# Graph attention on one core: scores of two units in a row as 64-row matmuls from the split halves, and all six units' probabilities turned by DMA

## What is computed

```python
h = relu(layernorm(x))
q, k, v = h @ Wq + bq, h @ Wk + bk, h @ Wv + bv      # split into 6 heads of 64
scores = q @ k.T / sqrt(64) + where(adj, 0, -9e15)    # 256 x 256 per head
ctx = softmax(scores) @ v                             # heads joined again: 256 x 384
out = x + ctx @ Wf + bf
```

## Time and profile before

| | us |
|---|---|
| median of 3 runs | 651.73 (651.4 to 652.34) |
| the profiled execution, its own time | 649.83 |
| its span, first to last instruction | 648.0 |
| granted TensorE clock, mean | 0.997 |

### The profile page before, as it was taken

One profiled execution on the slowest core, in us unless ns is written; L12 is line 12 of the kernel. 1 busy time (PEld: TensorE's weight loads), 2 busy tenths in 40 slices (PEclk: granted clock), 3 DMA queues, 4 the chain that ended last, 5 costly groups with the idle time before them and its releaser, 6 DMA issues.

```text
span 648.0 us, 18229 instructions
## 1 busy us (share of the span) xinstructions
PE 623.6 (96%) x6678; PEld 511.9 (79%) x6678; DVE 493.0 (76%) x1545; ACT 517.5 (80%) x1166; POOL 423.5 (65%) x465
## 2 busy tenths in 40 slices
PE   8787999999999999999999999999999999999985
PEld 7465888888888888888888888888888888888853
DVE  6777787787778778777777877777787777877764
ACT  3558888888888888888888888888888888888872
POOL 3556677676667767666776766677676676767531
PEclk9999999999999999999999999999999999999999
DMA  8317677777667668866777697687867877766554
GB/s 251 89 34 148 154 142 147 167 156 155 158 158 144 150 150 168 154 158 157 136 159 160 155 156 160 155 143 152 153 158 165 149 164 134 165 133 127 130 127 91
DMA packets 207690, 95.84 MB, mean 148 GB/s; under 512 B 152817, under 2 KB 207602, under 8 KB 207602
## 3 DMA queue, kind: packets, MB, share of 16 engines
q1 hardware_dynamic: 206400, 94.68, 69.5%
q10 hardware_dynamic: 1202, 0.01, 0.1%
HBM read 17.05 MB, written 12.58 MB: 46 GB/s over the span
## 4 chain that ended last, share of the span: by engine, by line
PE 87%; issue 3%; DMA 2%; POOL 2%; SPq 2%; DVE 2%; ACT 1%; POOLq 0%; ACTq 0%; DVEq 0%
PE ring L859 18%; PE ring L861 18%; PE ring L860 18%; PE scores L920 6%; PE scores L921 6%; PE probs_t L930 4%; PE ctx L948 3%; PE ring L960 3%; PE ctx L950 3%; PE ctx L949 3%; PE ring L875 3%; DMA w_raw<-in_L_gnn_Wk_dram 1%; SPq L305 1%; DMA heads<-split 1%; SPq L297 1%
## 5 line engine op out<-in xcount | busy, mean ns | idle before, releaser
L406 POOL TENSOR_TENSOR p_rows<-probs,p_rows 128x512 f16<-128x512 f32 x128 | 148.5, 1160 | 143.8 <-ACT p_rows L509 143.8
L643 DVE CUSTOM_DVE_ANT_0 logits<-scores,mask,logit_unscale 128x256 f32<-128x256 f32 x384 | 170.5, 482 | 90.6 <-PE scores L921 90.6
L499 ACT ACTIVATE probs<-logits,raised 128x256 f32<-128x256 f32 x384 | 174.2, 500 | 6.2
L859 PE MATMUL ring<-h_hi,w_hi 128*128 128x256 f16 x576 | 157.1, 273 | 0.4 <-DVE w_lo L741 0.4
L861 PE MATMUL ring<-h_hi,w_lo 128*128 128x256 f16 x576 | 157.0, 272 | 0.0
L860 PE MATMUL ring<-h_lo,w_hi 128*128 128x256 f16 x576 | 156.9, 272 | 0.0
L390 POOL TENSOR_TENSOR split<-qk,split 128x512 f16<-128x512 f32 x96 | 111.7, 1164 | 42.1 <-DVE split L667 42.1
L521 ACT ACTIVATE qk<-ring,qk_bias_s,qkv_ratio 128x256 f32<-128x256 f32 x192 | 97.2, 557 | 5.4 <-PE ring L861 2.6
L948 PE MATMUL ctx<-v_hi,p_cols 128*128 128x65 f16 x768 | 89.1, 194 | 10.2 <-DMA p_cols<-p_rows 5.6
L920 PE MATMUL scores<-heads 128*128 128x256 f16 x384 | 94.3, 273 | 3.9 <-DMA heads<-split 3.9
L921 PE MATMUL scores<-heads 128*128 128x256 f16 x384 | 94.2, 273 | 0.0
(11 more groups left out here) (97 smaller groups left out, 1406.9 us busy)
## 6 DMA issues: line engine op xcount, KB each, us to landing
heads<-split SPq DMA_DIRECT2D x192, 96.0 KB, 2.2
x_in<-in_x_dram SPq DMA_DIRECT2D x32, 384.0 KB, 3.5
heads<-split SPq DMA_DIRECT2D x192, 64.0 KB, 2.1
out_dram<-result SPq DMA_DIRECT2D x64, 192.0 KB, 2.3
adj_in<-in_adj_dram SPq DMA_DIRECT2D x32, 64.0 KB, 2.3
p_cols<-p_rows SPq DMA_TRANSPOSE x128, 3.2
w_raw<-in_L_gnn_Wq_dram SPq DMA_DIRECT2D x1, 576.0 KB, 5.7
w_raw<-in_L_gnn_Wk_dram SPq DMA_DIRECT2D x1, 576.0 KB, 7.5
```

The source lines that it names most:

```text
L406: pool.tensor_tensor(p_rows[u][:, 1], probs[u % 3][:], p_rows[u][:, 0], ALU.subtract).then_inc(p_lo_ready, 1)
L499: act.activation(probs[u % 3][:, a], logits[u % 3][:, a], ACT.Exp, bias=raised[u % 3][:, a:a + 1], scale=-1.0).then_inc(probs_ready, 1)
L643: dve.tensor_tensor_reduce(out=logits[u % 3][:, a], in0=score_bank[u % 2][:, a * S:(a + 1) * S], in1=mask[b.parity][:, t], scale=logit_uns ...
L859: pe.matmul(out_ap, a_hi, m_hi, start=first, stop=False)
```

## The change

The four stacking DMAs a pair, the `heads` buffers and their zeros go. `split` gets a second copy by parity of the batch. `scores` now works for a group of two units (g = 0, 1, 2: units 2g and 2g+1) and is issued in `attend(0)`, `attend(2)` and `attend(4)`: for each unit three products (q_hi k_hi, q_hi k_lo, q_lo k_hi), each as two matmuls of 64 rows, head 0 from partitions 0 to 63 into bank 0, head 1 from partitions 64 to 127 into bank 1. A unit's parity picks the half of the bank. The group waits until VectorE has read all the units of the group before. All six units are split before they are turned, and turned by DMA; the transposes on TensorE, ScalarE's and VectorE's work on `pt_bank` go, and ScalarE's `probs_hi` of units 0 and 3 now stands right behind their `exps`.

```diff
-PE_UNITS = (0, 3)
+    GROUPS = UNITS // 2
-        split = [sb(f"split{j}", [P, 4, S], F16) for j in range(C)]
-        heads = [sb(f"heads{p}", [P, HEADS, 3, S], F16) for p in range(2)]
+        split = [[sb(f"split{p}_{j}", [P, 4, S], F16) for j in range(C)] for p in range(2)]
@@ SyncE
-            def place_heads(b, j):
-                wait(sp, qk_hi_ready, b.count(C, j + 1))
-                wait(sp, qk_lo_ready, b.count(C, j + 1))
-                for a in range(2):
...
-                    sp.dma_start(dst[own], src[own, 1:4]).then_inc(heads_placed[j], 16)
-                    sp.dma_start(dst[other, 0:2], src[own, 0:3:2]).then_inc(heads_placed[j], 16)
             def transpose_probs(b, u):
-                if u in PE_UNITS:
-                    return
-                wait(sp, p_lo_ready, b.count(len(DMA_UNITS), nth_dma(u)))
+                wait(sp, p_lo_ready, b.count(UNITS, u + 1))
@@ GpSimd
             def probs_lo(b, u):
-                if u in PE_UNITS:
-                    return
-                wait(pool, p_hi_ready, b.count(len(DMA_UNITS), nth_dma(u)))
+                wait(pool, p_hi_ready, b.count(UNITS, u + 1))
@@ ScalarE
             def exps(b, u):
-                if u < 3:
-                    if (b + -1).exists():
-                        probs_read(act, b + -1, u + 3)
-                else:
-                    probs_read(act, b, u - 3)
+                wait(act, p_lo_ready, b.count(UNITS, u - 2))
             def probs_hi(b, u):
-                if u in PE_UNITS:
-                    wait(act, pt_ready, b.count(len(PE_UNITS), nth_pe(u)))
-                    act.activation(p_cols[u][:, 0].rearrange("p a s q -> p (a s q)"), pt_bank[:],
-                                   ACT.Copy).then_inc(pt_hi_ready, 1)
-                    return
@@ VectorE
-                wait(dve, scores_ready, b.count(UNITS, u + 1))
+                wait(dve, scores_ready, b.count(GROUPS, u // 2 + 1))
-                        out=logits[u % 3][:, a], in0=score_bank[u % 2][:, a * S:(a + 1) * S],
+                        out=logits[u % 3][:, a], in0=score_bank[a][:, u % 2 * S:(u % 2 + 1) * S],
-            def probs_lo(b, u):
-                if u not in PE_UNITS:
-                    return
...
@@ TensorE
-            def scores(b, u):
-                t, j = u // C, u % C
-                if t == 0:
-                    wait(pe, heads_placed[j], b.count(4 * 16, 4 * 16))
-                wait(pe, logits_ready, b.count(2 * UNITS, 2 * u - 2))
...
+            def scores(b, g):
+                for u in (2 * g, 2 * g + 1):
+                    if u < C:
+                        wait(pe, qk_hi_ready, b.count(C, u + 1))
+                        wait(pe, qk_lo_ready, b.count(C, u + 1))
+                wait(pe, logits_ready, b.count(2 * UNITS, 4 * g))
+                for u in (2 * g, 2 * g + 1):
+                    t, tile = u // C, split[b.parity][u % C]
+                    for n, (q, k) in enumerate(((1, 2), (1, 3), (0, 2))):
+                        for a in range(2):
+                            own = slice(D * a, D * a + D)
+                            mm = pe.matmul(score_bank[a][:, u % 2 * S:(u % 2 + 1) * S],
+                                           tile[own, q, t * P:(t + 1) * P], tile[own, k],
+                                           start=(n == 0), stop=(n == 2))
                 mm.then_inc(scores_ready, 1)
-            def transpose_probs(b, u):
...
@@ TensorE, attend(u)
-                    if here:
-                        scores(b, u)
+                    if here and u % 2 == 0:
+                        scores(b, u // 2)
...
-                    if here and u - 1 in PE_UNITS:
-                        transpose_probs(b, u - 1)
```

More of the change, by code:

```diff
@@ L61, in gnn_attention @@
     UNITS = QT * C
-    DMA_UNITS = [u for u in range(UNITS) if u not in PE_UNITS]
+    GROUPS = UNITS // 2
     LAG = 4
@@ L254, in cycles @@
                 cycle(Batch(k))
[L256 to L264, removed]
-            if u in PE_UNITS:
-                wait(eng, pt_ready, b.count(len(PE_UNITS), nth_pe(u)))
-            else:
-                wait(eng, p_lo_ready, b.count(len(DMA_UNITS), nth_dma(u)))
         x_v = x.rearrange("b (t p) h -> b p t h", p=P)
@@ L576, in cycle @@
                     exps(b, 0)
+                    probs_hi(b, 0)
                 if here:
@@ L585, in cycle @@
                     v_hi_part(b, 1)
-                if here:
-                    probs_hi(b, 0)
                 if front:
@@ L600, in cycle @@
                     exps(b, 3)
+                    probs_hi(b, 3)
                 if front:
@@ L606, in cycle @@
                     probs_hi(b, 4)
-                    probs_hi(b, 3)
                 if b.k == 0:
@@ L750, in _ @@
                 dve.memset(v_hi[p][:, :, :, D:V1], 1.0).then_inc(ones_ready, 1)
-                for a in range(2):
-                    other = slice(D - D * a, 2 * D - D * a)
-                    dve.memset(heads[p][other, a:HEADS:2, 2], 0.0).then_inc(zeros_placed, 1)
             layer_stats(Batch(0), (0, 1))
@@ L816, in cycle @@
                     qk_hi_part(b + 1, 0)
-                if here:
-                    probs_lo(b, 0)
                 if before:
@@ L843, in cycle @@
                     weights_lo(3, 8)
-                if here:
-                    probs_lo(b, 3)
                 if before:
@@ L909, in project_v @@
                     mm.then_inc(v_ready, 1)
-            def scores(b, u):
-                t, j = u // C, u % C
-                if t == 0:
-                    wait(pe, heads_placed[j], b.count(4 * 16, 4 * 16))
-                wait(pe, logits_ready, b.count(2 * UNITS, 2 * u - 2))
-                for a in range(2):
-                    h = heads[b.parity][:, 2 * j + a]
-                    q = h[:, 0, t * P:(t + 1) * P]
-                    o = score_bank[u % 2][:, a * S:(a + 1) * S]
-                    pe.matmul(o, q, h[:, 1], start=True, stop=False)
-                    mm = pe.matmul(o, q, h[:, 2], start=False, stop=True)
-                mm.then_inc(scores_ready, 1)
@@ L924, in transpose_probs @@
-            def transpose_probs(b, u):
-                wait(pe, pt_lo_ready, b.count(len(PE_UNITS), nth_pe(u) - 1))
-                for a in range(2):
-                    wait(pe, probs_ready, b.count(2 * UNITS, 2 * u + a + 1))
-                    for s in range(QT):
-                        o = (a * QT + s) * P
-                        mm = pe.transpose(pt_bank[:, o:o + P], probs[u % 3][:, a, s * P:(s + 1) * P], ident[:])
-                mm.then_inc(pt_ready, 1)
+            def scores(b, g):
[12 more added lines that the diff above has]
+                                           start=(n == 0), stop=(n == 2))
+                mm.then_inc(scores_ready, 1)
@@ L933, in apply_probs @@
             def apply_probs(b, u):
                 t, j = u // C, u % C
-                if u in PE_UNITS:
-                    wait(pe, pt_lo_ready, b.count(len(PE_UNITS), nth_pe(u)))
-                else:
-                    wait(pe, p_placed[u], b.count(16, 16))
+                wait(pe, p_placed[u], b.count(16, 16))
                 if u == 0:
@@ L1001, in _ @@
             pe.wait_ge(peaks_joined, 1)
-            spread_peaks(pt_bank, slice(4, 5))
+            spread_peaks(peak_bank, slice(4, 5))
             def cycle(b):
@@ L1061, in cycle @@
                     project_v(b + 1, 1)
-            pe.wait_ge(zeros_placed, 4)
             cycles(cycle)
```

34 lines of the change are left out of this document (6 added, 28 removed).

## The result

The kernel after takes 620.2 us (median, 619.76 to 622.47) where the kernel before took 651.57 us (650.65 to 652.34) beside it on the same chip. The ratio is 0.9527, 95% interval 0.9505 to 0.955. The profiled execution took 620.36 us, its span is 618.4. Forecast were 619.5 us in a range of 602 to 640: it holds. By its own time the profiled execution fell by 29.5 us (649.83 to 620.36), not by the 32.2 of the sum. The other 1.9 us of the 31.4 between the medians come from which execution was profiled: that of before lay 1.7 us under its median of 651.57, that of after 0.2 above its own. The granted clock goes with this: of the 19 executions of before that were timed beside experiments 1 to 4, the five with a mean clock of 0.997 took 649.2 to 649.7 us, and those with 0.992 took 650.7 to 652.6.

The account below looks back on a forecast made before the run. TensorE's matmul stream was taken as the bound: 18.88 - 0.94 - 0.65 + 0.60 = 17.89 us a batch. Over 29 batches 28.7, plus 2.5 and 1.0, is 32.2 us less: median 651.73 to 619.5, range 602 to 640.

Parts of the forecast that it names:

- the 32.2 of the sum: Whole profiled execution: 28.7 us less from 29 full cycles, 2.5 from the fill, 1.0 from the drain; 649.83 becomes 617.6.
- TensorE's sum: TensorE's matmul stream in a full batch: 18.88 - 0.94 - 0.65 + 0.60 = 17.89 us.
- The turns: Transposes of two units a batch leave TensorE, 0.47 us each: -0.94 us a batch.
- A pair: Two 64-row score matmuls on different array halves overlap wholly, costing one 0.109 us: 18 pairs, -0.65 us a batch.
- The ways in and out: TensorE switching to 64 rows and back around each score group: 0.10 us each, six a batch, +0.60 us.
- the scores' forecast (-0.05): TensorE's new scores a batch: -0.65 us from overlapping matmuls and +0.60 for switching to 64 rows and back.
- The chain: ScalarE and VectorE steps from turned context to `h_lo`: 6.1 us with the semaphore, just fits TensorE's path of 6.15.
- the rival of free switches: On TensorE, switching to 64 rows costs nothing; the ScalarE-VectorE path to `h_lo` binds at 17.45 us a batch, 606.7 us; chance 0.22.
- ScalarE, GpSimd, VectorE: Their load a batch: ScalarE about 16.2 us, GpSimd 15.40, both under 17.89; VectorE loses work; GpSimd and VectorE cost 0.
- another engine: ScalarE and GpSimd, in fixed order behind each other, lose 2 us to waits: 18.4 us a batch, 634 us; chance 0.06.
- SyncE and DMA: DMA queue: twelve stacking DMAs a batch go, two transposes come; some 3 us stay before `apply_probs`, cost 0.
- Fill and drain: First and last batches: fill -2.5 us (bounds -7 and -1), drain -1 us (bounds 0 and -2).

Follow-up runs that it names:

- experiment 1: The kernel before with all six units turned by DMA, stacked heads and 128-row scores kept: 674.65 us, ratio 1.0372.
- experiment 2: The kernel before with the new 64-row scores and no stacking DMAs, units 0 and 3 still turned on TensorE: 650.87 us, ratio 1.000.
- experiment 3: The kernel after with each unit's three matmuls of head 0 first, then the three of head 1: 621.22 us, ratio 0.9565.
- experiment 4: The kernel after with each group's second unit behind `apply_probs`, so six switches to 64 rows and back a batch: 651.32 us, ratio 1.0013.
- experiment 5: The kernel after with one unused VectorE operation of 0.55 us ahead of `h_lo_part`: 638.14 us, ratio 0.9803.
- experiment 6: The kernel after with scores in two groups of three units a batch, two switches in and out instead of three: 632.2 us, ratio 0.9704.
- experiment 8: GpSimd normalises batch 2's x behind the first cycle's mask and lo halves: kernel after 620.71 us; two groups of three units 630.01, with unit 5 masked early 613.79.
- the groups of three with the mask early: The kernel after with scores in two groups of three units and VectorE masking unit 5 right behind unit 4: 616.31 us, ratio 0.9482.

## Why the prediction was right

- **TensorE's sum.** 17.89 us a batch forecast, 17.93 measured. The turns gave 0.94 (experiment 2 to after). A pair costs 0.109, whole overlap. The ways in and out cost 3 x (0.096 + 0.093) = 0.57, forecast 0.60 from the single-row matmuls: a hole seen on float32 with one row held for float16 with 64. The first step of a group is 0.01 longer, 0.03 a batch. The steps inside `apply_probs` add up to 2.02 us a batch where they were 1.99, 0.03 more. With the 0.03 that the ways cost less, that is, to 0.01, what lies between the scores' forecast (-0.05) and experiment 2 (-0.01).
- **The chain.** That a chain of 6.1 us "just fits" into a path of 6.15 was the sharpest step: room of 0.05 forecast, 0.08 measured, 0.6 and 0.56 for before. From the last matmul that turns the context, the chain takes 6.14 us before and 6.15 after, while TensorE's own way to the q, k product fell from 6.76 to 6.29. Experiments 4, 5 and 6 show that it is the next bound, as the rival of free switches said.
- **ScalarE, GpSimd, VectorE.** 16.2, 15.40 and cost 0 forecast; the window has 15.87 and 15.23, and no TensorE wait. The rival "another engine" didn't come.
- **SyncE and DMA.** Right for the whole change, as TensorE has no wait for `p_placed`. But "The stacking itself was on no path in the full cycles" hides what experiment 1 shows. Without the removal of the stacking DMAs the two added transposes would have cost more than they give. The prediction looked at the new load of this queue only as a sum of both parts.
- **Fill and drain.** This is the term that was mis-sized: -2.5 and -1.0 forecast. Measured: the first full `transpose_h` at 71.76 against 73.30, -1.5. From the last listed one to the end, 62.43 us against 64.88, less two shorter cycles, -0.55. Together with 0.04 x 29 of the period that is about the 2.7 us between 32.2 and 29.5.
- **Luck in the median.** The profiled time was forecast at 617.6 and came at 620.36, 2.7 us off. The forecast of the median, 619.5, is only 0.7 off because it added the 1.9 us by which the profiled run of before lay under its median, and after has no such distance. That cancels 2.0 of the 2.7.

What the drain fell short by is the clock, as a second trace shows. Here is one window of 3.4 us in the kernel after and in experiment 3, whose scores of the last batch start at the same distances from its last `transpose_h` to within 0.02 us:

```profile
599.00:602.40 3.40, 3.40 (x26) 1.81 (x23) 1.83 (x9) 3.27 (x8) 2.23 (x2) 0.50 0.83 146
```

```profile
599.00:602.40 3.40, 2.46 (x33) 1.70 (x33) 3.12 (x14) 3.27 (x9) 1.74 (x3) 1.00 0.80 172
```

The kernel after is at 0.50, the 1.2 GHz level, after TensorE was busy for 6.48 of the 9 us before; experiment 3 stays at 1.00 there after 7.43 of 9. From the start of the last `transpose_h` to the end are 44.5 us in the first and 43.3 in the second. In the kernel before they were 46.0, with the clock at 1.00 to the end, and 0.95 of the difference is one shorter cycle. So the drain saves 1.7 us without that stretch and 0.5 with it, where 1.0 was forecast.

What took the place of the removed waits in the fill: TensorE's waits from 20 to 75 us, and a window of that stretch with its clock.

```profile
PE ctx L872 <- DMA p_cols<-p_rows: 4.7, 2, 3.1
PE ring L791 <- DVE w_lo L680: 3.4, 1, 3.4
```

```profile
45.00:50.00 5.00, 3.33 (x22) 1.85 (x21) 4.15 (x13) 4.49 (x9) 5.00 (x5) 0.60 0.87 181
```

The waits for heads (3.9 us in the earlier trace rows) are gone, those for turned probabilities grew from 2.3 to 4.7, and a wait of 3.4 for `w_lo` is new. GpSimd has two lo halves more in the first cycle and is busy for all 5 us of the window, but it was that before too, so that they are the cause is argued; with GpSimd's order changed (experiment 8) the wait for turned probabilities left this list and the time stayed. The clock is at 0.60 in this window, in part at the 1.2 GHz level, after TensorE was busy for only 1.93 of the 5 us before. The kernel before had 1.00 in the same window, after 4.23 of 5. How much of the 1.0 us missing in the fill is the clock stays open.

## What to carry to other kernels

A wait that vanishes from a profile may have been replaced by room of 0.08 us. Look at the distance from the last producer's end to the consumer's start and compare it with the distance when the consumer really waits (0.06 here): that tells what the next saving can bring. Count an edit also by what it frees on a shared queue. The scores alone gave nothing, the turn alone lost 3.7%, both together gained 4.7%. Where two engines feed a chain, bring the chain's own step ahead of work that nobody waits for before shortening the bound engine: the groups of three lost 0.39 us a batch without that and won 0.21 with it.

## What was unexpected in the hardware

- 64-row matmuls on the two halves of the array cost 0.109 us a pair whatever their order is within a unit: the two start 3 ns apart when the halves alternate, 10 ns when three of one half stand ahead of three of the other. That the later one overtakes in the second case is argued, not shown.
- Going from 128 to 64 rows and back costs 0.096 and 0.093 us each time, on float16 at the full clock.
- A DMA transpose lands in 3.1 us in the median, but right behind an x load it takes 3.8 to 5.9 us, and in six batches of the groups of three with the mask early 6.4 to 6.9.
- A stretch of 3.4 us at the 1.2 GHz level in the drain cost 1.1 us.
